# The down product of a feed-forward layer, turned round: weights stand, tokens move

## The reference, cut to what matters

```python
x = x + tanh(g_xattn[0]) * L0_xattn(layernorm(x), ctx)   # a recurrence over each sequence
x = x + tanh(g_ffn[0])   * L0_ffn(layernorm(x))          # the second block, below
x = x + tanh(g_xattn[1]) * L1_xattn(layernorm(x), ctx)   # linear attention
x = x + tanh(g_ffn[1])   * L1_ffn(layernorm(x))          # eight experts, two of them for each token

def L0_ffn(h):                    # h: tokens by 256
    mlp = silu(h @ gate_w) * (h @ up_w) @ down_w          # 256 -> 1024 -> 256
    # routing picks 8 of 512 one-row experts for a token
    ew = silu(h . down_embed[i]) * softmax(scores)        # 8 weights
    return mlp + sum(ew * up_embed[i])
```

## Time and profile before

| | |
|---|---|
| runs | 519.1, 519.27 and 519.87 us; median 519.27 |
| profiled execution, first to last instruction | 517.5 us |
| around the span, to the median | 1.8 us |
| PE busy | 449.8 us, 87% |
| DVE busy | 360.9 us, 70% |
| ACT busy | 246.7 us, 48% |
| POOL busy | 154.5 us, 30% |
| mean granted clock of TensorE | 0.967 |

### The profile page before, as it was taken

The page is one execution under the profiler, slowest core; times in us unless marked ns, Lnnn a source line. Parts: engine busy times, 40 slices in busy tenths (PEclk is TensorE's granted clock), DMA queues, the critical chain, the costliest instruction groups (busy, mean ns, idle before and its releaser), DMA issues. The chain is left out here.

```text
span 517.5 us, 7233 instructions
## 1 busy us (share of the span) xinstructions
PE 449.8 (87%) x2142; PEld 355.1 (69%) x2142; DVE 360.9 (70%) x1034; ACT 246.7 (48%) x452; POOL 154.5 (30%) x156
## 2 busy tenths in 40 slices
PE   1617999599999889999999999898999799899991
PEld 1315688368578666878778886787777588788851
DVE  6896779995289986565987966978867554531173
ACT  3618574363576346346125315470453454955540
POOL 3955342330002131110000001032336014477771
PEclk9966999799999989999999999999999999999997
DMA  8500312000300000960000000123232423346394
GB/s 303 187 31 30 103 31 83 0 1 0 101 2 0 2 0 14 310 178 0 1 1 1 1 0 2 32 71 102 90 115 83 123 73 91 114 139 208 85 385 153
DMA packets 32965, 42.00 MB, mean 81 GB/s; under 512 B 3483, under 2 KB 26781, under 8 KB 32928
## 3 DMA queue, kind: packets, MB, share of 16 engines
q1 hardware_dynamic: 28224, 32.28, 20.7%
q0 software_dynamic: 3744, 8.42, 4.4%
q10 hardware_dynamic: 960, 0.86, 0.5%
HBM read 24.97 MB, written 18.39 MB: 84 GB/s over the span
## 5 line engine op out<-in xcount | busy, mean ns | idle before, releaser
L660 PE MATMUL acc<-w_down,act_s 128*128 128x256 f32 x384 | 92.2, 387 | 0.9 <-DVE act_s L1386 0.9
L660 PEld LDWEIGHTS acc<-w_down,act_s 128*128 128x128 f32 x384 | 74.6, 195 | 13.2 <-DVE act_s L1386 1.3
L636 PE MATMUL ring<-xt_h,up_l 128*128 128x512 f32 x160 | 70.5, 441 | 2.9 <-DVE xt_l L1356 1.5
L1601 POOL TENSOR_TENSOR rstd<-var_eps,minus_half 128x4 f32<-128x4 f32 x14 | 14.9, 1068 | 176.5 <-DVE var_eps L1186 176.5
L637 PE MATMUL ring<-xt_l,up_h 128*128 128x512 f32 x160 | 63.8, 399 | 0.0
L638 PE MATMUL ring<-xt_h,up_h 128*128 128x512 f32 x160 | 63.7, 398 | 0.0
L1098 ACT ACTIVATE act_s<-ring 128x512 f32<-128x512 f32 x48 | 28.6, 597 | 59.9 <-PE ring L638 59.6
L631 PE MATMUL ring<-small,xn 128*128 128x128 f32 x160 | 23.6, 297 | 26.2 <-ACT xn L998 14.1
L699 PE MATMUL ring<-up_e,act_s 128*128 x184 | 44.3, 383 | 2.3 <-issue 2.0
L1637 POOL DMA_INDIRECT x_rows<-main_a,slots x32 | 31.1, 971 | 43.7 <-ACT main_a L1119 34.8
L1390 DVE TENSOR_TENSOR act_s<-ring,act_s 128x512 f32<-128x512 f32 x32 | 22.0, 686 | 30.8 <-PE ring L638 21.0
(11 more groups left out here) (275 smaller groups left out, 987.8 us busy)
## 6 DMA issues: line engine op xcount, KB each, us to landing
main_b<-x_rows SPq DMA_DIRECT2D x22, 257.0 KB, 2.8
x_rows<-v_t SPq DMA_DIRECT2D x1, 3983.5 KB, 16.7
up_l<-y_rows SPq DMA_DIRECT2D x5, 512.0 KB, 7.0
stage<-in_w_mlp SPq DMA_DIRECT2D x8, 256.0 KB, 2.6
up_e<-in_w_moe SPq DMA_DIRECT2D x8, 256.0 KB, 2.6
x_rows<-v_t SPq DMA_DIRECT2D x1, 1927.5 KB, 22.8
x_nat<-in_x SPq DMA_DIRECT2D x7, 256.0 KB, 7.7
out_x<-x_nat SPq DMA_DIRECT2D x6, 256.0 KB, 5.2
```

Source lines behind the costliest of these rows:

```text
L636: pe.matmul(out, wl, xh, start=first, stop=False, skip_group_check=True)
L660: last = pe.matmul(acc[t // 2][:, t % 2, :], act_s[n % RING][:, tok], w_down[:, u, :], start=u == 0 and t % 2 == 0, stop=final, skip_group ...
```

## The change

The operands of `down` change places. The down weights of a unit stand, in two halves of 128 columns, and the 512 tokens of the hidden block move. Both are split into a high part (a float32r copy, made by ACT) and a low part (the rest, made by POOL), and each half is a `three_pass`. `acc` then holds features on the partitions and tokens along the row. `mlp_out` gets two parts: in part 0 ACT copies both `acc` tiles to `host_s`, in part 1 PE transposes them in eight pieces of 128 by 128 into two ring banks, and DVE adds from there. To make room, `picks` and `exps` are kept once instead of once for each routing group.

```diff
-        13: "mlp 0 14 15, mlp_in 1 2, route_in 1 1 2",
+        13: "mlp 0 14 15, mlp_in 1 2, route_in 1 1 2, mlp_out 0 0",
...
-        1: "mlp_out 0 0, kv 1 3 4, route 1 0, kv 2 0",
+        1: "mlp_out 0 1, kv 1 3 4, route 1 0, kv 2 0",
...
-LAST = """mlp_out 3 0, attn_in 3 0, shared 0 0 1, shared 1 0, shared 2 0, attn_in 3 1, shared 1 1, shared 2 1,
+LAST = """mlp_out 3 0, shared 0 0 1, mlp_out 3 1, attn_in 3 0, shared 1 0, shared 2 0, attn_in 3 1, shared 1 1, shared 2 1,
...
-        acc = [ctx.enter_context(nc.psum_tensor(f"acc{k}", [P, 2, D], F32)) for k in range(2)]
+        acc = [ctx.enter_context(nc.psum_tensor(f"acc{c}", [P, GN], F32)) for c in range(C)]
...
-                hidden_made(pe, n)
-                final = u == MLP_UNITS - 1
-                for t in range(GT):
-                    tok = slice(t * P, (t + 1) * P)
-                    last = pe.matmul(acc[t // 2][:, t % 2, :], act_s[n % RING][:, tok], w_down[:, u, :],
-                                     start=u == 0 and t % 2 == 0, stop=final, skip_group_check=True)
+                pe.wait_ge(hid_low, n + 1)
+                pe.wait_ge(down_low, n + 1)
+                first, final = u == 0, u == MLP_UNITS - 1
+                xh, xl, wh, wl = hid_h[n % LAG], hid_l[n % RING], down_h[n % 2], down_l[n % 2]
+                for c in range(C):
+                    cols = slice(c * P, (c + 1) * P)
+                    last = three_pass(acc[c][:, :], wh[:, cols], wl[:, cols], xh[:, :], xl[:, :], first, final)
...
+                elif kind == "mlp_out" and part == 1:
+                    pe.wait_ge(acc_free, C * (g + 1))
+                    for p in range(2):
+                        key = (step, "M", p)
+                        bank = open_bank(key)
+                        for t in range(2):
+                            for c in range(C):
+                                tok = slice((2 * p + t) * P, (2 * p + t + 1) * P)
+                                last = pe.transpose(bank[:, (t * C + c) * P:(t * C + c + 1) * P], host_s[:, c, tok], ident)
+                        close_bank(key, last)
...
+            def split_down(n):
+
+                if n >= 2:
+                    act.wait_ge(down_done, n - 1)
+                act.activation(down_h[n % 2][:, :], w_down[:, n % MLP_UNITS, :], ACT.Copy).then_inc(down_high, 1)
+
+            def split_hidden(n):
+
+                hidden_made(act, n)
+                if n >= LAG:
+                    act.wait_ge(down_done, n - LAG + 1)
+                act.activation(hid_h[n % LAG][:, :], act_s[n % RING][:, :], ACT.Copy).then_inc(hid_high, 1)
...
                 elif kind == "mlp":
                     u = part - 1
+                    n = unit_of(g, u)
+                    if 0 <= u - 2 < MLP_UNITS:
+                        split_down(n - 2)
+                    if 0 <= u - 1 < MLP_UNITS:
+                        split_hidden(n - 1)
...
+                elif kind == "mlp_out" and part == 0:
+                    act.wait_ge(down_done, (g + 1) * MLP_UNITS)
+                    for c in range(C):
+                        act.activation(host_s[:, c, :], acc[c][:, :], ACT.Copy).then_inc(acc_free, 1)
...
-                elif kind == "mlp_out":
-                    dve.wait_ge(down_done, (g + 1) * MLP_UNITS)
+                elif kind == "mlp_out" and part == 1:
                     for p in range(2):
                         b = main_seqs(g)[2 * p]
-                        residual(x_nat[:, b:b + 2, :], acc[p][:, :, :], 1).then_inc(acc_free, 1)
-                    dve.wait_ge(acc_free, 2 * (g + 1))
+                        bank = full(dve, (step, "M", p))
+                        free((step, "M", p), residual(x_nat[:, b:b + 2, :].rearrange("p t d -> p (t d)"), bank[:, :], 1))
...
+                elif kind == "mlp":
+                    n = unit_of(g, part - 1)
+                    if 0 <= part - 3 < MLP_UNITS:
+                        pool.wait_ge(down_high, n - 1)
+                        k = (n - 2) % 2
+                        pool.tensor_tensor(down_l[k][:, :], w_down[:, part - 3, :], down_h[k][:, :].bitcast(F32),
+                                           ALU.subtract).then_inc(down_low, 1)
+                    if 0 <= part - 2 < MLP_UNITS:
+                        pool.wait_ge(hid_high, n)
+                        low = (n - 1) % RING
+                        pool.tensor_tensor(hid_l[low][:, :], act_s[low][:, :], hid_h[(n - 1) % LAG][:, :].bitcast(F32),
+                                           ALU.subtract).then_inc(hid_low, 1)
```

More of the change, by code:

```diff
@@ L311, in build @@
         wqg = sb("wqg", [P, C, 2 * D])
-        picks = sb("picks", [P, NG, 4, TOPK + NK], BF16)
-        exps = sb("exps", [P, NG, 4, TOPK + NK + 1])
+        picks = sb("picks", [P, 4, TOPK + NK], BF16)
+        exps = sb("exps", [P, 4, TOPK + NK + 1])
         sel_picks = sb("sel_picks", [P, EC, P], BF16)
@@ L359, in build @@
         xt_f = xt_f_pad[:, 0:C * GN].rearrange("p (c n) -> p c n", c=C)
-        act_s = [sb(f"act_s{k}", [P, GN]) for k in range(RING)]
+        hid_l, act_s = [], []
+        for k in range(RING):
+            with nc.sbuf_tensor(f"hid_l{k}", [P, GN], F32R) as low:
+                hid_l.append(low)
+            act_s.append(sb(f"act_s{k}", [P, GN]))
+        hid_h = [sb(f"hid_h{k}", [P, GN], F32R) for k in range(LAG)]
+        down_h = [sb(f"down_h{k}", [P, D], F32R) for k in range(2)]
+        down_l = [sb(f"down_l{k}", [P, D], F32R) for k in range(2)]
         host_s = sb("host_s", [P, 2, GN])
@@ L465, in build @@
         hid_ready = sem("hid_ready")
+        hid_high = sem("hid_high")
+        hid_low = sem("hid_low")
+        down_high = sem("down_high")
+        down_low = sem("down_low")
         down_done = sem("down_done")
@@ L599, in xt_wait @@
                 eng.wait_ge(bank_full[k], turn)
-        key_iota_f = exps[:, 2:4, :, :].rearrange("p g r k -> p (g r k)")[:, 0:GN]
+        key_iota_f = kv_sum[:, NSEQ - 2:NSEQ, :].rearrange("p b m -> p (b m)")[:, 0:GN]
         sel_picks_f = kv_sum[:, NSEQ - 4:NSEQ - 2, :].rearrange("p b m -> p (b m)")[:, 0:EC * P]
@@ L804, in _ @@
                     for r in range(4):
-                        last = pe.transpose(half_words[:, r * P:(r + 1) * P], picks[:, rg, r, :], identb[:, :])
+                        last = pe.transpose(half_words[:, r * P:(r + 1) * P], picks[:, r, :], identb[:, :])
                     close_bank(key, last)
@@ L809, in _ @@
                     for r in range(4):
-                        last = pe.transpose(bank[0:TOPK + NK + 1, r * P:(r + 1) * P], exps[:, rg, r, :], ident)
+                        last = pe.transpose(bank[0:TOPK + NK + 1, r * P:(r + 1) * P], exps[:, r, :], ident)
                     close_bank(key, last)
@@ L1045, in _ @@
                     act.activation(pair_d[:, :, :], pair_d[:, :, :], ACT.Exp)
-                    act.activation(exps[:, g, :, 0:TOPK + NK], exps[:, g, :, 0:TOPK + NK], ACT.Exp).then_inc(exp_ready, 1)
+                    act.activation(exps[:, :, 0:TOPK + NK], exps[:, :, 0:TOPK + NK], ACT.Exp).then_inc(exp_ready, 1)
                 elif kind == "mlp_in" and part == 2:
@@ L1295, in _ @@
                                       pair_top[:, :, 0:1].broadcast_to([P, 4, TOPK * TOPK]), ALU.subtract)
-                    dve.tensor_tensor(exps[:, g, :, 0:TOPK], logits[:, 0:4, 0:TOPK],
+                    dve.tensor_tensor(exps[:, :, 0:TOPK], logits[:, 0:4, 0:TOPK],
                                       top_v[:, 0:4, 0:1].broadcast_to([P, 4, TOPK]), ALU.subtract)
-                    dve.tensor_tensor(exps[:, g, :, TOPK:TOPK + NK], logits[:, 4:8, :],
+                    dve.tensor_tensor(exps[:, :, TOPK:TOPK + NK], logits[:, 4:8, :],
                                       top_v[:, 4:8, 0:1].broadcast_to([P, 4, NK]), ALU.subtract).then_inc(diff_ready, 1)
@@ L1314, in _ @@
                     with nc.allow_low_precision("counts up to 8 are exact in bfloat16"):
-                        link(dve.tensor_reduce(picks[:, g, :, 0:TOPK], hot, AX_X, ALU.add))
+                        link(dve.tensor_reduce(picks[:, :, 0:TOPK], hot, AX_X, ALU.add))
                 elif kind == "route" and part in (6, 7):
@@ L1327, in _ @@
                     with nc.allow_low_precision("ranks up to 8 are exact in bfloat16"):
-                        link(dve.tensor_reduce(picks[:, g, 2 * a:2 * a + 2, TOPK:], onehot[:, :, :, :], AX_X, ALU.add))
+                        link(dve.tensor_reduce(picks[:, 2 * a:2 * a + 2, TOPK:], onehot[:, :, :, :], AX_X, ALU.add))
                 elif kind == "route" and part == 8:
@@ L1337, in _ @@
                     zb = r_z[:, :].unsqueeze(2).broadcast_to([P, 4, TOPK])
[L1338 removed]
+                    dve.tensor_tensor(exps[:, :, 0:TOPK], exps[:, :, 0:TOPK], zb, ALU.mult)
                     link(dve.tensor_tensor(r_sum[:, :, :], r_sum[:, :, :], zb, ALU.mult))
@@ L1342, in _ @@
                                                   ALU.is_ge, ALU.mult))
```

(2 more changed lines are left out.)

5 lines of the change are left out of this document (1 added, 4 removed), and 8 rows, old and new, of the table PLAN.

## The result

The changed kernel takes 564.78 us (median of 564.14 to 565.72), the kernel before 519.57 beside it: a ratio of 1.085, 95% interval 1.0816 to 1.0883. It is slower by 8.5%, 45 us; I had forecast 527, 515 to 538. The profiled execution has a span of 563.0 us. In what follows a hundredth of a ratio is put at 5.2 us; by the intervals a difference of two ratios is then good to between 1 and 4 us.

The account below looks back on a forecast made before the run. The prediction took TensorE to bound the main groups, with VectorE ahead of two waits and POOL at group 3's end. -13.8 + 2.6 + 3.3 + 3 + 3.6 + 1 + 5.9 + 1.9 = +7.5 us gave 527, range 515 to 538.

Parts of the forecast that it names:

- a shorter matmul there should be felt: Main groups, 100 to 390 us: PE busy 278.0 of 290 us, so shorter matmuls should shorten the time.
- -13.8 + 3.3 = -10.5 us: Down products: 42 units at 0.33 us save 13.8; 3.3 of it is lost in longer PE waits.
- the two waits of the earlier trace: PE's 5.25 and 3.82 us waits ahead of first expert units for VectorE's routing; 3.3 us of saving lost there.
- The interface cost: Main groups: POOL's low parts slow VectorE by 9 us through shared SBUF interfaces, 3 reaching the time.
- Part 10: Group 3: unit 6's low weights stand behind four scatters, so its down product starts 4.0 us later, 3.6 on.
- Unit 10: End of group 3: low parts behind the sixth scatter; PE idle about 7 us, last down product ending 5.4 later.
- The first expert product: Tail after group 3: comes 5 to 8 us later after the row numbers of `place 2` than 18.3 us.
- The scatters of the next parts are too few to add more: Group 3, after part 8's four scatters: later scatters on POOL's queue add no further delay.
- 3.6 + 5.4 + 1.9 + 1: POOL's queue: part 10 delay 3.6, end of group 3 5.4, halved clock there 1.9, slower clock after part 10 1.
- ACT's copies: High-part copies in every unit: 48 us on ACT, costed at 0; a failing silu cover, 10 us, left to the range.
- The tail and transposes: Eight new transposes a group, 2.6 us for three groups; copies and transposes at the end, 0.5.
- The rival that VectorE becomes the bound: Main groups: VectorE's 9 us reach PE in full and ACT's cover fails in a few units; 535.8 us, chance 0.23.

Follow-up runs that it names:

- the kernel with the saving alone: Six float32r matmuls a unit as in the changed kernel, no splitting work, VectorE writing the hidden block as float32r, fixed weight blocks; 518.33 us, ratio 0.9964.
- the powers: Changed kernel with each low-part subtraction on POOL replaced by a 128 by 4 power in the same place, high parts used for low; 546.80 us, ratio 1.0487.
- the order: Kernel with powers in place of low parts, POOL's table of steps also rewritten so fewer late steps stand ahead; 531.57 us, ratio 1.02.
- without low parts: Changed kernel with both POOL subtractions gone, PE taking ACT's high parts for the low ones, six matmuls kept; 527.63 us, ratio 1.0125.
- three pairs of runs: ACT's silu put ahead of its copies: in the changed kernel 563.65 us; with POOL's low parts gone 524.18; with POOL's order rewritten 550.14.
- The two runs with one kind of copy: Kernel with no POOL low parts, ACT keeping the hidden block's copies (weights copied for two units only), 523.40 us; or the weights' copies only, 520.95 us.
- the float32 version: Changed kernel with the down product turned round but in float32, two matmuls a unit, no high or low parts; 522.90 us, ratio 1.002.
- the table of four ratios: Turned-round float32 down product 1.0020, with VectorE's rank work replaced by a small copy 0.9895; six float32r matmuls without splitting 0.9964, with that relief 0.9746.

## Why the prediction was wrong

**The size of PE's saving was right, its arrival was not.** A down product took 1.73 us before; the starts of its matmuls are 0.231 us apart after (the median), so six take 1.39, 0.34 off where I had 0.33. The step that failed is "a shorter matmul there should be felt", read from PE's 278 of 290 us. Of -13.8 + 3.3 = -10.5 us, about -2.9 arrive (-4.6 by the medians). I let the two waits of the earlier trace rows take the saving of the five units ahead of each, 10 in all; in fact the second takes all that was gained up to it, the later units of group 0 included. And in group 2, where PE was busy 98% before (windows 214 to 308), little is gained either: the kernel with the saving alone is 1.2 us ahead at unit 1 and still 1.2 at unit 7. In these 39.9 us PE's busy time falls by 1.2 us, from 38.75 to 37.58, and its idle time rises by as much, from 1.15 to 2.32. So a PE that was almost never idle was paced by the others all the same. The Trainium skill (Perfetto Trace Analysis, Identifying the Most-Contended Engine) says that TensorE's matmul busy share is not a good measure of how close one is to roofline. The run with the saving alone agrees that the share misleads: 278 of 290 us hid that others set the pace. The page's reason, that pipelined instructions look smaller in the trace, is not what is seen here.

**The interface cost was mis-sized: 3 us taken, bounds 0 and 9; VectorE's busy time rose by 23.0 and the time by 18.9.** The mechanism was right, as the powers show; both factors of the term were too small. I priced 0.13 of VectorE's time at 1.5 us a pair of instructions, 9 us, with the scans and the normalizing as what is struck; it is 23.0. The scans of the earlier trace rows carry none of it and the normalizing 3.7 us. What is struck most are operations with both inputs in SBUF (L1428, L1365 and L1368 alone 3.9, 3.3 and 2.5 us more than before). And I let a third of it reach the time; by the table the cost grows in every group, by 5.5, 4.0, 5.9 and 5.3 us.

**POOL's order was right in the two places that I worked out, and missed elsewhere.** Part 10: 4.01 us of waiting where I had 4.0. Unit 10: 5.19 us, where I had about 7 of idle time ahead of it and 5.4 for the end of the last product. The twelve matmuls behind it are 0.43 us apart instead of 0.23, at a granted clock of 0.50 (the level of 1.2 GHz) until 440.0: 2.4 us where I had 1.9. The window of the changed kernel, the clock third from the end:

```profile
434.70:440.00 5.30, 5.26 (x13) 4.18 (x14) 0.00 (x0) 0.00 (x0) 3.75 (x4) 0.50 0.15 53
```

The first expert product starts 26.7 us after the row numbers, 8.4 later than before, where I had 5 to 8. The step that failed is that the order costs nothing elsewhere ("The scatters of the next parts are too few to add more"): I looked at POOL's scatters alone and not at its layernorm steps, whose wait for VectorE cost PE 4.66 us at the end of group 2. POOL's queue as a whole cost 18.8 us where my terms for it (3.6 + 5.4 + 1.9 + 1) made 11.9; 14.9 came back with the order.

**ACT's copies were taken as 0 and cost 8.4 us.** I had left 10 us of it to the range, as a silu behind a late copy. The silu was late, as that sentence said, but most of its wait is not the copies': VectorE waits 16.7 us for it without low parts and still 11.4 with the matmuls' saving alone, where ACT copies no more than two blocks of weights. Putting the silu first gave back 1.9 to 3.1 us in three pairs of runs, each with intervals that overlap. The two runs with one kind of copy point to ACT's 50 us of new work. Without low parts PE waits 2.8 us for the copies of the weights themselves; where the rest of the 8.4 is lost stays open.

**The tail and transposes.** 2.6 us and 0.5 us for copies and transposes at the end were expected; the float32 version has 2.6 by the spans, 1.0 by the ratio.

The sum of what was measured, in ratio steps, beside what I had forecast:

| term | forecast, us | measured, us |
|---|---|---|
| turned round: transposes, copies of the sums | +3.1 | +1.0 |
| PE's saving, less what doesn't arrive | -10.5 | -2.9 |
| ACT's copies | 0 | +8.4 |
| POOL's queue, with the clock behind its waits | +11.9 | +18.8 |
| the interface of VectorE and POOL | +3 | +18.9 |
| sum | +7.5 | +44.2 |

The rival that VectorE becomes the bound was nearest, at 535.8 us: it had the mechanism and a third of its size. What each step is worth depends on the order in which they are taken away, as the table of four ratios shows. The lower mean clock, 0.925 against 0.967, goes with the waits, as in the window above; what it costs by itself was not measured.

## What to carry to other kernels

Before pricing a saving on an engine that looks full, run the kernel with that saving and none of its costs, with parts of the computation left out where need be: here the most that the change could bring was 3 to 5 us, and its helpers cost 46. Long work given to POOL was paid by VectorE here, most of all in the operations that read two tiles in SBUF, so list those instructions one by one. In a queue that is served in order, look ahead of each moved step for every wait, not only for the long transfers.

## What the runs showed of the hardware

In these rows, of VectorE and POOL the one that comes second waits for the other. In the changed kernel ten of the sixteen products L1428 take 0.69 us. Here is another, beside two subtractions, DVE and then POOL:

```profile
406.12 2.36 DVE L1428 TENSOR_TENSOR act_s<-act_s,host_s 128x512 f32<-128x512 f32 x1
```

```profile
405.95 0.74 POOL L1667 TENSOR_TENSOR down_l<-w_down,down_h 128x256 fp32r<-128x256 f32 x1
406.64 1.28 POOL L1672 TENSOR_TENSOR hid_l<-act_s,hid_h 128x512 fp32r<-128x512 f32 x1
```

POOL came first, and VectorE's product ends 0.56 us after both are done. The five others that started behind a subtraction, by 0.25 to 0.34 us, end 0.54 to 0.56 us after it. The other way round, in the same kernel:

```profile
109.40 0.69 DVE L1428 TENSOR_TENSOR act_s<-act_s,host_s 128x512 f32<-128x512 f32 x1
109.47 1.20 POOL L1667 TENSOR_TENSOR down_l<-w_down,down_h 128x256 fp32r<-128x256 f32 x1
```

VectorE came 0.07 us earlier, takes its 0.69, and POOL's subtraction takes 1.20 instead of 0.72. The Trainium skill (SBUF — State Buffer, SBUF: two separate sides) says that the shared pair of ports is an exclusive lock which whoever starts first keeps for the whole instruction; both orders agree. A power of 128 by 4 on POOL is an exception, though it too reads SBUF. In the kernel with powers a product that started 0.24 us behind a power took its 0.69 us all the same:

```profile
110.28 1.01 POOL L1670 TENSOR_TENSOR down_l<-pow_in,minus_half 128x4 f32<-128x4 f32 x1
```

```profile
110.52 0.69 DVE L1429 TENSOR_TENSOR act_s<-act_s,host_s 128x512 f32<-128x512 f32 x1
```

A power that started 0.08 us behind such a product, at 104.22, took 1.48 us instead of 1.01. So it waits like a subtraction, but nothing shows that it makes VectorE wait.

Even a product of 128 by 64, L1449 before and L1490 after, went from 225 to 732 ns on average:

```profile
L1449 DVE TENSOR_TENSOR chosen<-later,s_if 128x64 f32<-128x64 f32 x4 | 0.9, 225 | 0.1
```

```profile
L1490 DVE TENSOR_TENSOR chosen<-later,s_if 128x64 f32<-128x64 f32 x4 | 2.9, 732 | 0.1
```
